# Turning the score maxima on VectorE instead of TensorE and ScalarE, placed by four transfers per eight heads

## The reference

```
x_mod = _modulate(_ln(x), shift_msa, scale_msa)
k, q, v = split(x_mod @ w_qkv, 3)              # 16 heads of 16 channels
q = q / CH
w = softmax(einsum('bqhc,bkhc->bhqk', q, k))   # 256 queries x 256 keys per head
y = einsum('bhqk,bkhc->bqhc', w, v)
x = x + gate_msa[:, None] * (y @ w_proj + b_proj)
```

## Time and profile before

| what | value |
|---|---|
| time of three runs | median 1659.14 us (1659.01 to 1662.07) |
| time of the profiled execution | 1658.74 us |
| its span | 1656.7 us |
| PE busy over the span | 1604.1 us (97%) |
| PEld busy | 1438.6 us (87%) |
| DVE busy | 1273.6 us (77%) |
| ACT busy | 868.4 us (52%) |
| POOL busy | 483.9 us (29%) |
| share of PE in the chain that ended last | 73% |
| share of DVE in it | 15% |

### The profile page before, as it was taken

The page is one execution under the profiler, slowest core; times in us unless marked ns, Lnnn a source line. Parts: engine busy times, 40 slices in busy tenths (PEclk is TensorE's granted clock), DMA queues, the critical chain, the costliest instruction groups (busy, mean ns, idle before and its releaser), DMA issues.

```text
span 1656.7 us, 42822 instructions
## 1 busy us (share of the span) xinstructions
PE 1604.1 (97%) x14686; PEld 1438.6 (87%) x14686; DVE 1273.6 (77%) x2826; ACT 868.4 (52%) x1760; POOL 483.9 (29%) x638
## 2 busy tenths in 40 slices
PE   8999999999999998999999999999998999999998
PEld 7999999999999998677777777777767999999998
DVE  5788887676666676788888888888885777777775
ACT  3666664333333343677767777677765333333332
POOL 2333322131212222233434334343324221222211
PEclk9999999999999999999999999999999999999999
DMA  6600001000000001333333233333330111111111
GB/s 182 198 20 19 21 14 53 5 1 0 0 0 0 0 2 52 110 94 104 108 105 102 93 102 107 102 102 98 102 118 21 52 39 52 38 51 38 41 47 38
DMA packets 99581, 100.67 MB, mean 61 GB/s; under 512 B 13792, under 2 KB 90016, under 8 KB 99504
## 3 DMA queue, kind: packets, MB, share of 16 engines
q1 hardware_dynamic: 99344, 99.60, 19.3%
q0 software_dynamic: 160, 0.04, 0.1%
HBM read 38.62 MB, written 8.55 MB: 28 GB/s over the span
## 4 chain that ended last, share of the span: by engine, by line
PE 73%; DVE 15%; issue 8%; ACT 1%; DVEq 1%; POOL 1%; DMA 0%; ACTq 0%; SPq 0%; POOLq 0%
PE bank L207 58%; DVE C_negmax L1677 8%; PE bank L1494 5%; PE bank L329 3%; PE bank L1508 2%; DVE C_tmp L1713 1%; DVE a_h_lo L348 1%; PE bank L1543 1%; PE bank L1551 1%; PE bank L695 1%; DVE B_g_lo L980 1%; DVE C_ytok L1703 1%; DVE C_msplit L1685 1%; PE bank L399 1%; PE bank L189 1%
## 5 line engine op out<-in xcount | busy, mean ns | idle before, releaser
L1677 DVE TENSOR_REDUCE C_negmax<-bank 128x4 f32<-128x1024 f32 x256 | 313.3, 1224 | 71.7 <-PE bank L1494 71.3
L1615 ACT ACTIVATE C_probs<-bank 128x1024 f32<-128x1024 f32 x256 | 262.4, 1025 | 119.3 <-PE bank L1508 116.4
L969 ACT ACTIVATE B_g<-bank,B_bias 128x256 f32<-128x256 f32 x256 | 107.6, 472 | 217.4 <-PE bank L207 213.6
L969 ACT ACTIVATE D_g<-bank,D_bias 128x256 f32<-128x256 f32 x256 | 107.5, 471 | 214.6 <-PE bank L207 214.6
L296 POOL TENSOR_TENSOR m_rstd<-m_var,neghalf 128x2 f32<-128x2 f32 x64 | 50.1, 783 | 579.7 <-DVE m_var L287 299.7
L1494 PEld LDWEIGHTS bank<-C_kx,C_qs 64*128 64x128 f32 x1024 | 77.4, 186 | 112.5 <-DVE C_negmax L1677 80.2
L1494 PE MATMUL bank<-C_kx,C_qs 64*128 64x256 f32 x1024 | 129.6, 331 | 27.0 <-DVE C_negmax L1677 15.9
L207 PE MATMUL bank<-B_wt_w_hi,B_g_lo 128*128 128x256 f32 x512 | 146.3, 286 | 4.0 <-DVE B_g_lo L980 3.7
L207 PE MATMUL bank<-D_wt_w_hi,D_g_lo 128*128 128x256 f32 x512 | 146.6, 286 | 2.2 <-DVE D_g_lo L980 1.4
L207 PE MATMUL bank<-m_h_hi,B_wt_w_lo 128*128 128x256 f32 x512 | 147.1, 287 | 0.0
L207 PE MATMUL bank<-m_h_hi,D_wt_w_lo 128*128 128x256 f32 x512 | 146.9, 287 | 0.0
(11 more groups left out here) (249 smaller groups left out, 5037.5 us busy)
## 6 DMA issues: line engine op xcount, KB each, us to landing
C_qs<-C_q_hi SPq DMA_DIRECT2D x128, 128.0 KB
C_kx<-C_k_hi SPq DMA_DIRECT2D x128, 128.0 KB, 2.1
C_qs<-C_q_lo SPq DMA_DIRECT2D x64, 128.0 KB
C_kx<-C_k_lo SPq DMA_DIRECT2D x64, 128.0 KB, 2.0
C_gbc<-mod_rows SPq DMA_DIRECT2D x32, 256.0 KB, 3.3
D_gbc<-mod_rows SPq DMA_DIRECT2D x32, 256.0 KB, 3.3
out<-xres SPq DMA_DIRECT2D x32, 256.0 KB, 3.5
xres<-in_x SPq DMA_DIRECT2D x4, 1792.0 KB, 11.5
```

What stands on the lines that cost most here:

```text
L969: ins = eng.activation(g[u][:, d * S:(d + 1) * S], hbank[u][:, d * S:(d + 1) * S], func, bias=per_seq(bias1, 2 * u + d, b))
L1615: e_exp.by(eng.activation(probs[t % NP][:, :], stpair[:, :], ACT.Exp, scale=scl))
L1677: e_max.by(eng.tensor_reduce(m4[:, :, :, j], spair[:, :].rearrange("p (e q k) -> p e q k", e=2, q=TH), AX, ALU.max, negate=True))
```

## The change

VectorE takes over the turning. There is now one `msplit` tile of 128 x 64 for both halves, ordered so that each 32 columns hold 32 values (16 of w = 0, then 16 of w = 1) for one of the two queries of a partition. After the cast (now L1678) and the subtraction (now L1680) a VectorE transpose (L1685) turns all 64 columns in blocks of 32 x 32 into `mT[w]`. Since the blocks stay within 32 partitions, `mT` has the 16 wanted rows four times, once per group of 32 partitions, with 64 queries each. So `place_max` issues four DMAs of 16 rows x 64 columns where it issued one of 16 rows x 256. For the columns to come out in the order of the queries, partition p has to hold queries 2p and 2p+1: S0 to S7 now take every second column of `qs` as stationary operand. The first `max_split` also fills the unused half of `msplit` once. M0, M1, mc0 and mc1 are gone, with their entries in the tables, and TensorE's wait for the phase before moves from M0 to Y1a.

```
-                msplit = [sb(f"msplit{w}", [P, TH * 16]) for w in range(2)]
-                mrow = [sb(f"mrow{w}", [16, S], F32R) for w in range(2)]
+                BLOCK, QUADS = 32, P // 32
+                msplit = sb("msplit", [P, TH * BLOCK])
+                mT = [sb(f"mT{w}", [P, TH * BLOCK], F32R) for w in range(2)]
...
-                        "v": 29.29, "M0": 29.61, "S5": 29.92, ...
-                        "M1": 38.49, "ST2": 39.37, ...
+                        "v": 29.29, "S5": 29.92, ...
+                        "ST2": 39.37, ...
...
     def scores(b, t):
-                                                 qs[b.par][rows, t * S + qh * P:t * S + (qh + 1) * P],
+                                                 qs[b.par][rows, t * S + qh:(t + 1) * S:TH],
...
     def scores_t(b, t):
-                            eng.wait_ge(s_md[w][b.par], (b.pair + 1) * 16)
+                            eng.wait_ge(s_md[w][b.par], (b.pair + 1) * QUADS * 16)
...
-                    def max_t(b, w):
-                        e_mlo.wait(eng, b, w + 1)
-                        for qh in range(TH):
-                            ins = eng.transpose(mbank(f"M{w}")[0:16, qh * P:(qh + 1) * P],
-                                                msplit[w][:, qh * 16:(qh + 1) * 16], ident[:, :])
-                        e_mT.by(ins)
...
-                        if b.reg is None and (name, b.off) == ("M0", 0):
+                        if b.reg is None and (name, b.off) == ("Y1a", 0):
                             prev.e_res.wait(eng, LAST)
...
-                    def max_row(b, w):
-                        e_mT.wait(eng, b, w + 1)
-                        prev = b.back(1)
-                        if not prev.before_first():
-                            eng.wait_ge(s_md[w][prev.par], (prev.pair + 1) * 16)
-                        e_mrow.by(eng.activation(mrow[w][:, :], mbank(f"M{w}")[0:16, 0:S], ACT.Copy))
...
     def max_split(b, w):
                         e_max.wait(eng, b, 4 * w + 4)
-                        e_mT.wait(eng, b.back(1), w + 1)
+                        if w == 0:
+                            e_mT.wait(eng, b.back(1), 2)
+                        else:
+                            e_mT.wait(eng, b, 1)
                         m3 = negmax[w][:, :].rearrange("p (q e t) -> p q e t", q=TH, e=2)
-                        s5 = msplit[w][:, :].rearrange("p (q e c t) -> p q e c t", q=TH, e=2, c=2)
-                        e_mhi.by(eng.tensor_copy(s5[:, :, :, 0].bitcast(F32R), m3))
+                        s6 = msplit[:, :].rearrange("p (q w e c t) -> p w q e c t", q=TH, w=2, e=2, c=2)
+                        if b.reg is None and b.off == 0 and w == 0:
+                            s_first = msplit[:, :].rearrange("p (q w m) -> p w q m", q=TH, w=2)
+                            e_mhi.wait(eng, b, 0)
+                            eng.tensor_copy(s_first[:, 1].bitcast(F32R), negmax[w][:, 0:1].unsqueeze(2).broadcast_to([P, TH, 16]))
+                        e_mhi.by(eng.tensor_copy(s6[:, w, :, :, 0].bitcast(F32R), m3))
                         e_mhi.wait(eng, b, w + 1)
-                        e_mlo.by(eng.tensor_tensor(s5[:, :, :, 1], m3, s5[:, :, :, 0], ALU.subtract))
+                        e_mlo.by(eng.tensor_tensor(s6[:, w, :, :, 1].bitcast(F32R), m3, s6[:, w, :, :, 0], ALU.subtract))
+                        e_mlo.wait(eng, b, w + 1)
+                        prev_b = b.back(1)
+                        if not prev_b.before_first():
+                            eng.wait_ge(s_md[w][prev_b.par], (prev_b.pair + 1) * QUADS * 16)
+                        e_mT.by(eng.transpose(mT[w][:, :].bitcast(F32).rearrange("p (r q) -> p q r", q=TH),
+                                              msplit[:, :].rearrange("p (q m) -> p q m", q=TH)))
...
     def place_max(b, w):
-                        e_mrow.wait(eng, b, w + 1)
-                        eng.dma_start(half(qs, b, w, ROW_MAX), mrow[w][:, :].bitcast(F32)).then_inc(s_md[w][b.par], 16)
+                        e_mT.wait(eng, b, w + 1)
+                        n = TH * BLOCK
+                        for quad in range(QUADS):
+                            p0 = quad * BLOCK + w * 16
+                            eng.dma_start(half(qs, b, w, ROW_MAX)[:, :, quad * n:(quad + 1) * n],
+                                          mT[w][p0:p0 + 16, :].bitcast(F32)).then_inc(s_md[w][b.par], 16)
```

More of the change, by code:

```diff
@@ L1305, in phase_l1_attention @@
                 e_max, e_exp = event("max", NT), event("exp", NT)
-                e_mhi, e_mlo, e_mT, e_mrow = (event(n, 2) for n in ("mhi", "mlo", "mT", "mrow"))
+                e_mhi, e_mlo, e_mT = (event(n, 2) for n in ("mhi", "mlo", "mT"))
                 e_av = event("av", 4)
@@ L1316, in phase_l1_attention @@
                 T_PE = {"T": 0.39, "q": 5.79, "k": 9.20, "S0": 19.86, "S1": 23.32, "S2": 24.33, "S3": 25.58, "S4": 28.26,
[2 rows of a table removed]
[2 rows of a table added]
                         "ST6": 46.46, "Y1a": 46.57, "ST7": 48.41, "AV2": 48.80, "AV3": 51.54, "Y1b": 53.19, "Y2": 57.19,
                         "PR": 63.70}
-                T_ACT = {"hi_h": 0.00, "hi_q": 6.62, "hi_k": 9.42, "mc0": 27.12, "vout": 27.97, "exp0": 32.35,
-                         "exp1": 32.97, "mc1": 34.51, "exp2": 34.98, "exp3": 39.01, "exp4": 41.38, "Y0": 41.93,
+                T_ACT = {"hi_h": 0.00, "hi_q": 6.62, "hi_k": 9.42, "vout": 27.97, "exp0": 32.35,
+                         "exp1": 32.97, "exp2": 34.98, "exp3": 39.01, "exp4": 41.38, "Y0": 41.93,
                          "exp5": 42.32, "exp6": 44.20, "exp7": 45.99, "Y1": 48.47, "hi_y": 56.55}
@@ L1338, in phase_l1_attention @@
                 NEXT_SP = {"D w2": 532, "D gates": 553, "D gates1": 554}
-                BANK = {"T": 2, "q": 2, "k": 1, "v": 2, "M0": 0, "M1": 0, "Y1a": 0, "Y1b": 1, "Y2": 0, "PR": 1}
+                BANK = {"T": 2, "q": 2, "k": 1, "v": 2, "Y1a": 0, "Y1b": 1, "Y2": 0, "PR": 1}
                 pe_order = schedule(0, T_PE)
@@ L1353, in phase_l1_attention @@
                 norm = Norm(attention_norm, event, False, scale1a, mbank("T"), (e_v, 1), centred=True)
-                freed = {"M0": (e_mrow, 1), "M1": (e_mrow, 2), "v": (e_vev, 1), "Y1a": (e_ytok, 1), "Y1b": (e_ytok, 2),
+                freed = {"v": (e_vev, 1), "Y1a": (e_ytok, 1), "Y1b": (e_ytok, 2),
                          "T": (norm.e_lo, 1), "Y2": (e_yf, 1), "q": (e_loq, 1), "k": (e_lok, 1), "PR": (e_tmp, 1)}
@@ L1572, in tensor @@
                              "k": lambda b: qk_cm(eng, b, "k"), "v": v_tok,
-                             "M0": lambda b: max_t(b, 0), "M1": lambda b: max_t(b, 1),
                              "Y1a": lambda b: y_tok(b, 0), "Y1b": lambda b: y_tok(b, 1), "Y2": y_chan, "PR": project}
@@ L1646, in scalar @@
                              "hi_k": lambda b: hi_bias(eng, b, "k"),
-                             "vout": v_out, "mc0": lambda b: max_row(b, 0), "mc1": lambda b: max_row(b, 1),
+                             "vout": v_out,
                              "Y0": lambda b: y_out(b, 0), "Y1": lambda b: y_out(b, 1), "hi_y": hi_y}
```

## The result

| | before | changed |
|---|---|---|
| median of nine runs | 1659.65 us (1657.93 to 1662.07) | 1663.8 us (1661.07 to 1665.39) |
| span of the profiled execution | 1656.7 us | 1660.4 us |
| time of the profiled execution | 1658.74 us | 1662.7 us |
| matmuls | 14686 | 14558 |
| ACT busy | 868.4 us | 852.5 us |

The ratio is 1.0022, with a 95% interval of 1.0012 to 1.0033. The time forecast was 1661.0.

What follows compares the result with a forecast made beforehand. It took each period to be bound partly by TensorE, partly by VectorE. Per sequence +0.27 (ms1) - 0.21 (M0), all else 0, gave +0.06 us; times 32, +1.9 us, so 1661.0 us, range 1656 to 1671.

Steps and rivals of the forecast that it cites:

- M0, -0.21: TensorE's part of the period, between v and S5: removing this transpose pair brings S5 0.21 us earlier per sequence.
- M1, nothing: VectorE's part of the period: removing this transpose pair gains nothing, since S1 waits for max0 either way (0.28 us).
- The transpose, 0.25 us long, +0.27 at ms1: On VectorE's chain after the subtraction: the added transpose takes 0.25 us and delays max0 by 0.27 us a sequence.
- The transpose at ms0, nothing: VectorE while max4 waits for S4: starts 0.04 us after the subtraction, delays max4 some 0.05, within slack, costing nothing.
- The rival in which GpSimd holds it up: At ms0, GpSimd's normalising delays the VectorE transpose: +0.15 to +0.37 us a sequence, about 1668 us; chance 0.09.
- The DMAs, nothing: SyncE: four issues of about 0.59 us replace one, twice a sequence; landing about 2.1 us, within slack, costing nothing.
- The strided load, nothing: Weight loads of S0 to S7 taking every second column stay at 0.184 us, adding zero.
- one of the forecast's own signs of being wrong: Prediction wrong if S's weight loads lengthen, transpose exceeds 0.35 or is under 0.17, ST0/S4 waits for DMA, or TensorE's clock falls.
- The rival's mechanism: S's weight loads: the stride halves the rate, +0.10 us a load, +0.6 a sequence, +19 us, 1680; chance 0.09.
- within 0.2%: Whole-kernel time within about 0.2%, 3.3 us, of no change: chance 0.46, against slower 0.41 and faster 0.13.
- the forecast's own case: Transpose at 0.16 to 0.36 and M0 at 0.21: -0.03 to +0.19 us a sequence, 1658 to 1665 us; chance 0.60.
- ScalarE, nothing: Two copies a sequence removed from ScalarE, which has over a quarter of its time free and is off the chain: zero.

Runs made afterwards that it cites:

- the kernel with the keys ahead: Changed kernel with the keys k1 issued ahead of the maxima transfers md1 on SyncE: 1662.44 us, ratio 1.0017 to the kernel before, period 18.854 us.
- the late ms1: Changed kernel with ms1 moved behind max0 and the second division on VectorE: 1657.99 us, ratio 0.9988 to the kernel before.

## Why the prediction was right, and where its sum was off

**What bounds the kernel, and the sign.** The period has a part of TensorE and a part of VectorE, and a piece of work is worth what the part says in which it falls. Shown: a second, equal transpose costs 0.098 us at ms1 and 0.010 at ms0, and the one at ms1 is worth 0.309 when it is left out. The one at ms0 was not left out by itself. The sign of the forecast is right and so is its mechanism; the size, +1.9 us, is about half of what was measured (+3.6 by the periods).

**M0, -0.21.** Right. S5 now follows v by 0.21 us, as S3 follows k, in the timeline of TensorE:

```profile
902.77 0.28 PE L207 MATMUL bank<-C_wt_v_hi,a_h_hi 128*128 128x256 f32 x1
902.98 0.51 PE L1495 MATMUL bank<-C_kx,C_qs 64*128 64x256 f32 x4
```

Doubling the pair costs 0.222.

**M1, nothing.** Right in its result, partly by luck: the slack behind it was 0.06 and not 0.28, as the doubled pair showed, and had M1 ended more than 0.06 us later, its removal would have been worth something.

**The transpose, 0.25 us long, +0.27 at ms1.** Its length is 0.246. In place it cost 0.29 by the timeline and 0.309 by the period of the kernel without it. The term was 0.02 to 0.04 too small: the transpose waits for the end of the subtraction, and max0 cannot start under the subtraction's tail any more.

**The transpose at ms0, nothing.** Right. It started 0.13 us after the subtraction's end in most sequences, not 0.04, for a reason that stays open, and it cost nothing all the same. The rival in which GpSimd holds it up fell, and not by the order of starts: in the changed kernel GpSimd began 0.05 to 0.08 ahead of the transpose in 11 of 32 sequences, and all 64 transposes had 0.245 to 0.249. The Trainium skill, "SBUF — State Buffer", gives the ports that VectorE shares with GpSimd to whoever starts first, but only where VectorE runs in a 2-port mode or has two SBUF inputs. The transpose has one input and was not held up even as the second to start; the subtraction has two, and its 0.62 and 0.66 us beside GpSimd agree. That condition is what the forecast's rival had left out.

**The DMAs, nothing.** Right for the steady loop: the kernel with the keys ahead has the same period, and in the changed kernel's loop neither S nor ST waits for a transfer. In the last sequence, outside the loop, one ST does, which none did before:

```profile
1258.97 0.33 PEld L1509 LDWEIGHTS bank<-C_qs,C_kx 64*128 64x128 f32 x4 [0.86 <-DMA C_qs<-C_mT]
```

What that costs in time was not tested. The four issues take 2.31 us and not 2.4. The landing was taken too lightly: 4.16 us has been seen where 2.1 was assumed, and this is what the late ms1 ran into.

**The strided load, nothing.** Wrong in size, and longer loads were one of the forecast's own signs of being wrong. The rival's mechanism was real at about a twelfth of its price: 8 ns a load in the steady loop (6 by the medians of the whole phase) instead of 100, and 0.04 to 0.06 us a sequence on the chain. The Trainium skill, "SBUF — State Buffer", in its note on SBUF cachelines, has such a step free; by these rows it is nearly so.

**The sum.** With the measured terms +0.31 - 0.22 + 0.05 = +0.14 a sequence, where the periods say +0.113; the forecast was +0.06. The two terms that were small by 0.04 and 0.05 explain the difference, and 0.03 too much; that rest was not traced. They moved the result from "within 0.2%", the likelier class, to 0.22%, and its interval reaches to both sides of 0.2%. The upper end of the forecast's own case was also added up wrongly: a transpose of 0.36 gives 0.38 - 0.21 = +0.17 a sequence and not +0.19.

**ScalarE, nothing.** It lost 16 us of busy time and the kernel became slower. Right.

## What to carry to other kernels

Before moving work from one engine to another, find for each place in the period which of the two is waited for; the change here took 0.2 us from a place where TensorE bound and put 0.3 where VectorE did. Then look for a place where the added work is free: two numbers in the order tables, ms1 and k1, made the same change worth 10 us instead of costing 4 (ms1 alone: 1 to 2), and nearly 15 with contiguous loads. Price an instruction by leaving it out rather than by doubling it, since a second one of its kind may overlap the first. Effects below the scatter of the times are resolved by the period of a steady loop in the trace.

## What the runs showed of the hardware

- A VectorE transpose of 128 x 64 fp32 in 32 x 32 blocks takes 245 to 249 ns; a second one without a wait starts 0.17 us after the first and moves what follows by 0.12.
- It keeps that length beside a GpSimd operation, whichever of the two started first (11 of 32 sequences with GpSimd first).
- A weight load of 64 x 128 with a step of two elements takes 192 ns in the steady loop, where one without takes 184.
- S behind TensorE's transposes of the maxima has a gap of 0.22 us before its weight load, which the profile may put down to a wait for another engine, although that engine had finished 0.19 us before the load.
- VectorE's cast and subtraction of 16 columns, SBUF to SBUF, took 0.38 to 0.51 and 0.66 us beside GpSimd's additions, and 0.17 each when moved away from them.
- A transfer of 128 KB of keys landed 4.16 us after its issue, where the median is 2.1.
